# A decoder layer: the first sorted tiles set between the last token tiles, and the last two blocks' first-stage rows added by TensorE

## The chip, the cores and the metric

One core of a Trainium2 chip runs the whole layer in one launch. The metric is the device time of the kernel in microseconds (us). The core has five instruction queues: PE (TensorE, matmuls), DVE (VectorE), ACT (ScalarE), POOL (GpSimd, here mostly the indirect DMAs that scatter rows) and SP (SyncE, the other DMAs). Each runs its instructions in the order in which they are written; semaphores order the queues among each other.

## What is computed

The layer takes 4096 tokens (4 sequences of 1024) with 256 features. Three stages follow one another, each with a residual and a LayerNorm: a gated convolution with a scan (the first stage), three steps of slot attention with a GRU, in which the tokens are the slots, and a mixture of eight experts of which each token uses one:

```python
# GRU cell of the slot attention, three times
    r = jax.nn.sigmoid(xr + hr)
    z = jax.nn.sigmoid(xz + hz)
    n = jnp.tanh(xn + r * hn)
    return (1.0 - z) * n + z * h
...
# experts
    scores = jnp.einsum('bsh,eh->bse', x, gate_w)
    chosen = jnp.argmax(scores, axis=-1)
    onehot = jax.nn.one_hot(chosen, gate_w.shape[0], dtype=x.dtype)
    expert_out = jnp.einsum('bsh,efh->bsef', x, expert_w)
    return x + jnp.einsum('bsef,bse->bsf', expert_out, onehot)
...
    x = _layernorm(x + _L0_attn_ref(x, ...), axis=-1)
    x = _layernorm(x + _L0_xattn_ref(x, ctx_1024, ...), axis=-1)
    x = _layernorm(x + _L0_ffn_ref(x, L0_ffn_gate_w, L0_ffn_expert_w), axis=-1)
```

The second residual is what the change is about: the input of the experts is (first-stage rows + GRU slots), centred and scaled.

## The kernel before

**GRU units.** The slots are kept with features on partitions, in `full` (chunk c of 2, sequence b of 4). A pass k (of six) handles two sequences in eight units q = 0 to 7; a unit is one block of 512 tokens and one chunk of 128 features. For a unit PE runs the hidden and input matmuls of the gates R, HN, XN and Z (`unit`, line 1403), ACT the sigmoids and tanh, and DVE (`hidden_part` 1788, `input_part` 1795, `mix` 1806 to 1817) ends it with the new slots. `LAST` is the last pass; its units 4 and 5 finish block 6 (tokens of tiles 24 to 27), its units 6 and 7 block 7 (tiles 28 to 31). So a block is four token tiles.

**First-stage rows.** They wait in DRAM (`x1_scratch`) and are loaded block by block into the two buffers of `x1b`. The sum with the finished slots is made in place in `full`: for blocks 0 to 3 by POOL (`add_x1`), for blocks 4 to 6 by DVE (`add_block`, line 1892), and for block 7 in two halves, one per feature chunk (`add_half`, line 1900; the half of chunk 0 stands before unit 7 ends, that of chunk 1 behind it). Semaphore `w_mid` counts these sums.

**Token tiles.** `token_tile(n)` (line 1367) turns 128 tokens to rows: two matmuls, one per chunk, against `eyeg`, which holds the identity, the centred gate weights of the eight experts and a column of -1/256. It gives a PSUM bank with 128 + 9 columns per chunk. DVE adds the nine extra columns (`score`, 1839), ACT writes the centred row to `rowb` (`row`, 773) and squares it (`row_square`, 780).

**Sorting.** Tokens come in five groups: tiles 0 to 7, 8 to 15, 16 to 23, 24 to 27 and 28 to 31. Per group DVE picks the expert (`choose`), PE counts ranks (`ranks`, 1383 to 1385), DVE makes addresses (`destinations`, 1871 to 1875), and POOL sends each row by an indirect DMA to its expert's region in DRAM (`send_row`, 1014). After group 2 the first 15 sorted tiles of 128 rows (`NSOON`), filled from the first 24 token tiles alone, can be laid out: `soon_places` gives their rows, and SP gathers them (`gather`, 498) as soon as the rows of groups 0 to 2 have landed. The other 24 tiles need the counts of all groups: `first_counts` to `last_rows`, a chain of dependent small DVE instructions, then `base_set` 2, and the landing of all rows.

**Sorted tiles.** For each of 39 tiles, in order: `turn(i)` (PE transposes a gathered tile into PSUM, 1464), a copy to `wT` (ACT `copy_turned`, 787, for the first 15; DVE `copy_late`, 1997, for the rest), `expert(i)` (two matmuls against the weights of the expert plus identity, 1493, into one of six PSUM buffers), `statistics(i)` on DVE (2001, 2003). For each group of three (`TG`) follow `variance`, `out_index`, ACT's `inverse`, DVE's `offset` (2031), ACT's `normalise` (806), and POOL's `send_out` (1022). A PSUM buffer is free again when its row is normalised, six tiles later.

**The order around the change.** On PE: units 6 and 7 with tiles 24 to 27 inside, `ranks(3)`, tiles 28 to 31, `turn(0)`, then per i: `turn(i + 1)`, `expert(i)`, with `ranks(4)` behind expert(0). On DVE: four scores, `choose(4)`, `statistics(0)`, `destinations(4)`, and the counting chain with statistics 1 and 2 in it, statistics 3 to 5 behind it. On POOL: all 32 row sends, then all 39 output sends. The order is written out by hand; nothing plans it.

## Time and profile before

| | us |
|---|---|
| median of 3 runs | 594.06 |
| lowest, highest | 592.83, 597.93 |
| the profiled execution | 590.11 |
| its span in the trace | 588.3 |
| mean granted TensorE clock in it | 0.945 |

The profiled execution is a separate one; its span runs from the first to the last instruction, and 1.8 us lie around it. Times in the rows are from the span's start.
### The profile page before, as it was taken

The numbers are of one execution on the slowest core, as the hardware profiler recorded it, in microseconds if no ns is written. First come the engines' busy times: TensorE is split into PE (matmuls) and PEld (weight loads), VectorE is DVE, ScalarE is ACT, GpSimd is POOL, SyncE is SP. The second block draws the span as 40 slices with busy tenths as digits, with TensorE's granted clock in tenths as the row PEclk, the third lists the DMA queues.
The fourth block names the chain that finished last, engine by engine and source line by source line (L and its number), as shares of the span: only waits on it lengthen the run. The fifth ranks groups of instructions, "written<-read, shape, count | busy, mean of one in ns | idle before, by whom it ended". The sixth has DMA issues, their size and how long they took to land.

```text
span 588.3 us, 7233 instructions
## 1 busy us (share of the span) xinstructions
PE 519.0 (88%) x2158; PEld 372.4 (63%) x2158; DVE 439.7 (75%) x798; ACT 344.0 (58%) x608; POOL 240.4 (41%) x213
## 2 busy tenths in 40 slices
PE   6999896979779989999999999999899887987770
PEld 2466454737656865787688678768677766765550
DVE  2899999987996679799679859965956767655551
ACT  3657459775884746674676667456476635452322
POOL 0021030302132546559356555915433564564553
PEclk9999997989799989999999999999999988688985
DMA  8950202110001040000000000021121723454410
GB/s 297 297 169 2 72 1 74 70 71 1 37 36 73 0 145 0 2 0 2 0 1 0 1 0 2 0 72 36 36 72 40 270 77 106 132 170 122 135 67 28
DMA packets 28101, 39.98 MB, mean 68 GB/s; under 512 B 7421, under 2 KB 19838, under 8 KB 27776
## 3 DMA queue, kind: packets, MB, share of 16 engines
q1 hardware_dynamic: 24656, 31.10, 17.0%
q0 software_dynamic: 3408, 8.43, 4.0%
q8 instruction: 18, 0.29, 0.2%
q14 instruction: 19, 0.16, 0.1%
HBM read 25.70 MB, written 16.83 MB: 72 GB/s over the span
## 4 chain that ended last, share of the span: by engine, by line
PE 46%; DVE 13%; issue 7%; POOL 2%; another core or an unknown queue 2%; ACT 2%; POOLq 0%; DVEq 0%; ACTq 0%
PE psum L1403 32%; PE psum L1493 6%; PE psum L1234 2%; PE psum L1367 2%; PE psum L1464 2%; DVE gru L1815 2%; DVE slots_full L1817 1%; PE psum L1319 1%; DVE gru L1788 1%; DVE gru L1795 1%; POOL gru L984 1%; DVE slots_lo L1638 1%; PE psum L1331 1%; DVE st L2001 1%
## 5 line engine op out<-in xcount | busy, mean ns | idle before, releaser
L1403 PE MATMUL psum<-slots_hi,w_hh 128*128 128x512 f32 x560 | 182.5, 408 | 4.5 <-DVE gru L1788 4.5
L1403 PEld LDWEIGHTS psum<-slots_hi,w_hh 128*128 128x128 f32 x560 | 104.8, 192 | 32.1 <-DVE gru L1788 5.8
L1403 PE MATMUL psum<-slots_lo,w_hh 128*128 128x512 f32 x280 | 112.5, 402 | 0.0
L984 POOL TENSOR_TENSOR gru<-slots_full,gru 128x512 f32<-128x512 f32 x43 | 65.8, 1530 | 112.8 <-ACT gru L750 112.8
L1403 PE MATMUL psum<-at,v_ih_pair 128*128 128x512 f32 x288 | 92.6, 406 | 3.1 <-DVE at L1694 3.1
L750 ACT ACTIVATE gru<-gru,vec 128x512 f32<-128x512 f32 x48 | 34.6, 722 | 63.7 <-DVE gru L1795 63.5
L1403 PEld LDWEIGHTS psum<-at,v_ih_pair 128*128 128x128 f32 x288 | 54.7, 193 | 19.8 <-DVE at L1694 3.4
L1788 DVE SCALAR_TENSOR_TENSOR gru<-psum,vec,gru 128x512 f32<-128x512 f32 x48 | 35.9, 748 | 39.3 <-PE psum L1403 30.1
L1117 PE MATMUL psum<-early_hi,w_in 128*128 128x512 f32 x128 | 58.6, 618 | 5.1 <-DMA early_hi<-in_xT 5.1
L1403 PEld LDWEIGHTS psum<-slots_lo,w_hh 128*128 128x128 f32 x280 | 53.8, 192 | 12.9
L1493 PE MATMUL psum<-slots_full,w_tile 128*128 x156 | 49.3, 445 | 13.5 <-DVE w_tile L1997 9.2
L1022 POOL DMA_INDIRECT out<-out_tile,out_index x39 | 37.9, 972 | 32.0 <-ACT out_tile L806 19.5
L1117 PEld LDWEIGHTS psum<-early_hi,w_in 128*128 128x128 f32 x128 | 25.3, 199 | 36.0 <-issue 35.1
L1815 DVE TENSOR_TENSOR gru<-gru 128x512 f32<-128x512 f32 x48 | 42.9, 893 | 5.3 <-ACT gru L757 2.2
L999 POOL TENSOR_TENSOR slots_lo<-slots_full,slots_hi 128x512 fp32r<-128x512 f32 x32 | 46.6, 1456 | 0.6 <-DVE slots_hi L1822 0.6
L1817 DVE TENSOR_TENSOR slots_full<-gru 128x512 f32<-128x512 f32 x48 | 45.0, 937 | 1.7
L744 ACT ACTIVATE gru<-psum,brz 128x512 f32<-128x512 f32 x48 | 32.7, 681 | 22.6 <-PE psum L1403 22.4
L1014 POOL DMA_INDIRECT sorted_rows<-row_block,dest x32 | 33.4, 1043 | 27.9 <-DVE row_block L1885 10.4
L1493 PEld LDWEIGHTS psum<-slots_full,w_tile 128*128 128x128 f32 x156 | 30.7, 219 | 21.8 <-issue 18.1
L1795 DVE TENSOR_TENSOR gru<-psum,gru 128x512 f32<-128x512 f32 x48 | 33.2, 692 | 7.5 <-PE psum L1403 5.3
L993 POOL TENSOR_TENSOR ss_block<-sq_block 128x512 f32<-128x512 f32 x16 | 22.3, 1391 | 39.2 <-ACT sq_block L765 35.7
L757 ACT ACTIVATE gru<-psum,brz 128x512 f32<-128x512 f32 x48 | 32.5, 677 | 2.0 <-PE psum L1403 1.8
(239 smaller groups left out, 874.0 us busy)
## 6 DMA issues: line engine op xcount, KB each, us to landing
gathered<-sorted_rows SPq DMA_DIRECT2D x39, 129.0 KB
x_scratch<-slots_full SPq DMA_DIRECT2D x8, 512.0 KB, 3.0
x_block<-x_scratch SPq DMA_DIRECT2D x8, 512.0 KB, 4.0
early_hi<-in_xT SPq DMA_DIRECT2D x3, 1024.0 KB, 5.5
x_tm<-in_x SPq DMA_DIRECT2D x4, 512.0 KB, 7.2
slots_full<-expert_plus SPq DMA_DIRECT2D x1, 2048.0 KB
sorted_rows<-gru SPq DMA_DIRECT2D x1, 1032.0 KB, 11.7
early_hi<-in_xT SPq DMA_DIRECT2D x2, 512.0 KB, 4.3
```

The costliest lines, as they stand in the source:

```text
L750: act.activation(X(u), X(u), ACT.Tanh, bias=col(c, V_BIH + 2)).then_inc(n_act, 1)
L984: pool.tensor_tensor(DF(u), full[:, c, seq(k, h), blk(j)], X(u), ALU.subtract).then_inc(d_pool, 1)
L999: last = pool.tensor_tensor(slots[1][:, c, b, blk(j)], full[:, c, b, blk(j)], slots[0][:, c, b, blk(j)].bitcast(F32), ALU.subtract)
L1014: pool.indirect_dma_start(rows[:], bass.IndirectOffsetOnAxis(dest[:, n:n + 1], 0), rowb[:, row_slot(n), :], None, bounds_check=E * REGION - 1,
L1022: pool.indirect_dma_start(out[:], bass.IndirectOffsetOnAxis(oidx[:, g % 4, t:t + 1], 0), og[:, i % (4 * TG), :], None, bounds_check=TOK - ...
L1117: last = pe.matmul(psum[:, bank + j, :], wi[:, k, at_col:at_col + P], xF[b % 2][:, k, cols_of(j)], start=k == 0, stop=k == C - 1)
L1403: last = pe.matmul(psum[:, bank, :], w, d, start=start and i == 0, stop=stop and i == len(pairs) - 1, skip_group_check=begun or late)
L1493: last = pe.matmul(expert_out(i), wT[:, i % TG, c, :], ew[:, c, bass.ds(off, D)], start=c == 0, stop=c == C - 1)
L1788: dve.scalar_tensor_tensor(out=X(u), in0=psum[:, HN_B, :], scalar=col(c, V_BHH + 2), in1=X(u), op0=ALU.add, op1=ALU.mult).then_inc(t_dve, 1)
L1795: dve.tensor_tensor(X(u), psum[:, XN_B, :], X(u), ALU.add).then_inc(t2_dve, 1)
L1815: dve.tensor_tensor(Z(u), Z(u), DF(u), ALU.mult).then_inc(e_dve, 1)
L1817: dve.tensor_tensor(full[:, c, seq(k, h), blk(j)], X(u), Z(u), ALU.add).then_inc(s_dve, 1)
```

## The change

Four things change together. First, DVE's adds of blocks 6 and 7 go. Tiles 24 to 31 take the first-stage rows by two more matmuls out of `x1b` (`late_input`), accumulated in PSUM with the two out of the unsummed slots (`late_slots`). Second, on PE the input parts of tiles 28 to 31 stand ahead of `ranks(3)`, and their slot parts behind `turn(0)`, between the first sorted tiles; `ranks(4)` moves from behind expert(0) to behind expert(3). The first three gathers get a semaphore each, so that `turn(0)` waits for its own gather alone. Third, ACT and DVE follow this order: copies between the last rows, statistics between the last scores and through the counting chain. Fourth, POOL sends the first three outputs ahead of the rows of tiles 28 to 31.

```diff
@@ block.sync
-                    gather(i, places[i] if i < TG else row_of(i), gat_in[i // TG % 4])
+                    gather(i, places[i] if i < TG else row_of(i), gat_first[i] if i < TG else gat_in[i // TG % 4])
@@ block.scalar, normalise
-                        if g < NE and t < TG - 1 and TG * g + 6 + t < NSOON:
+                        if g == 0:
+                            copy_turned(5 + t)
+                        elif g < NE and t < TG - 1 and TG * g + 6 + t < NSOON:
                             copy_turned(TG * g + 6 + t)
@@ block.scalar
-                for n in range(28, 32):
-                    row(n)
-                copy_turned(0)
+                for i in range(TG):
+                    copy_turned(i)
+                    row(28 + i)
+                row(31)
                 row_square(28)
                 row_square(29)
-                copy_turned(1)
+                copy_turned(3)
                 row_square(30)
                 row_square(31)
-                for i in range(2, 5):
-                    copy_turned(i)
                 inverse(0)
-                copy_turned(5)
+                copy_turned(4)
                 normalise(0)
@@ block.gpsimd
-                for g, (t0, n) in enumerate(GROUPS):
+                def send_group(g):
+                    t0, n = GROUPS[g]
                     for t in range(t0, t0 + n):
                         send_row(t, g)
-                for i in range(NTL):
+
+                for g in range(NGRP - 1):
+                    send_group(g)
+                for i in range(TG):
+                    send_out(i)
+                send_group(NGRP - 1)
+                for i in range(TG, NTL):
                     send_out(i)
@@ block.tensor
+                def late_input(n):
+
+                    i = n // TJ
+                    pe.wait_ge(x1_in3[i % 2], 16 * (i // 2 + 1))
+                    token_bank(n)
+                    for c in range(C):
+                        pe.matmul(token_part(n, c), x1b[:, i % 2, c, token_cols(n, TJ)], eyeg[:, c, :],
+                                  start=c == 0, stop=False, skip_group_check=True)
+
+                def late_slots(n):
+                    b, i = n // NT, n // TJ
+                    for c in range(C):
+                        pe.wait_ge(s_dve, UL - QU + C * i + (c + 1 if i == 2 * B - 1 else C))
+                        last = pe.matmul(token_part(n, c), full[:, c, b, token_cols(n, NT)], eyeg[:, c, :],
+                                         start=False, stop=True, skip_group_check=True)
+                    last.then_inc(tile_mm, 1)
@@ block.tensor, turn
-                    if g == NE:
-                        pe.wait_ge(gat_first[t], 16)
+                    if g in (0, NE):
+                        pe.wait_ge(gat_first[t], 16 if g == 0 else 32)
@@ block.tensor
-                unit(LAST, 6, {"XN": tiles_after(24)})
-                token_tile(25)
-                unit(LAST, 7, {"R": tiles_after(26), "HN": tiles_after(27)})
+                unit(LAST, 6, {"XN": late_after(24)})
+                late_tile(25)
+                unit(LAST, 7, {"R": late_after(26), "HN": late_after(27)})
+                for n in range(28, 32):
+                    late_input(n)
                 ranks(3)
-                token_tile(28)
-                token_tile(29)
-                token_tile(30)
-                token_tile(31)
                 turn(0)
                 for i in range(NSOON):
                     off = offset_of(i)
+                    if i < TG:
+                        late_slots(28 + i)
+                    if i == TG - 1:
+                        late_slots(31)
                     if i + 1 < NSOON:
                         turn(i + 1)
                     expert(i, off)
-                    if i == 0:
+                    if i == TG:
                         ranks(4)
@@ block.vector
                 settle(LAST, 5)
-                add_block(6)
                 hidden_part(LAST, 6)
...
                 mix(LAST, 6, soon_passed)
-                add_half(0)
                 score(25)
...
                 settle(LAST, 7)
-                add_half(1)
                 destinations(3)
                 side(3)
-                for n in range(28, 32):
-                    score(n)
+                score(28)
+                statistics(0)
+                score(29)
+                statistics(1)
+                score(30)
+                score(31)
                 choose(4)
...
                 variance(0)
                 out_index(0)
-                last_counts(link)
+                side(4)
                 offset(0)
+                statistics(3)
+                destinations(4)
+                statistics(4)
+                first_counts(link)
+                statistics(5)
...
```

`token_tile` keeps its form for tiles 0 to 23; its waits for banks move unchanged into `token_bank(n)`, which `late_input` calls. `late_after(n)` and `late_tile(n)` run `late_input(n)` and `late_slots(n)` one behind the other. In the rest of DVE's new order `variance`, `out_index` and `offset` of groups 1 and 2 and statistics 6 to 8 stand between the parts of the counting chain, whose instructions are the same.

PE behind the last unit, before. `slots_full` with `eye_and_gate` is a token tile, `gathered` a turn, `w_tile` an expert.

```order
L1367 MATMUL psum<-eye_and_gate,slots_full 128x137 [waits t_dve,w_mid]
L1367 MATMUL psum<-eye_and_gate,slots_full 128x137
L1367 MATMUL psum<-eye_and_gate,slots_full 128x137 [waits t2_dve,w_mid]
L1367 MATMUL psum<-eye_and_gate,slots_full 128x137
L1464 MATMUL psum<-ident,gathered 128x128 [waits r_act,gat_in_0]
L1464 MATMUL psum<-ident,gathered 128x128
L1475 TENSOR_LOAD soon_off [waits more_set]
L1464 MATMUL psum<-ident,gathered 128x128 [waits turn_ev]
L1464 MATMUL psum<-ident,gathered 128x128
L1493 ISA [waits z_act,ew_in,turn_ev]
L1493 ISA x2
L1493 MATMUL psum<-slots_full,w_tile 128x256
```

After; `x1_block` is an input part (1391), `slots_full` with `eye_and_gate` a slot part (1398).

```order
L1420 MATMUL psum<-cum4_1,ones_f 128x32
L1499 MATMUL psum<-ident,gathered 128x128 [waits r_act,gat_first_0]
L1499 MATMUL psum<-ident,gathered 128x128
L1510 TENSOR_LOAD soon_off [waits more_set]
L1398 MATMUL psum<-eye_and_gate,slots_full 128x137 [waits s_dve] x2
L1499 MATMUL psum<-ident,gathered 128x128 [waits turn_ev,gat_first_1]
L1499 MATMUL psum<-ident,gathered 128x128
L1528 ISA [waits z_act,ew_in,turn_ev]
L1528 ISA x2
L1528 MATMUL psum<-slots_full,w_tile 128x256
L1528 ISA x2
L1528 MATMUL psum<-slots_full,w_tile 128x256
```

The turn of tile 0 has come ahead of all slot parts of tiles 28 to 31, and expert(0) stands behind one of them where it stood behind four tiles.

DVE behind the last row's side columns, before. `token_scores` is a score, `route_tmp`, `hot4` and `cum4` the choice, `st3` and `mv3` statistics.

```order
L1883 COPY row_block<-tok 128x4 [waits row_out_0]
L1885 TENSOR_SCALAR row_block<-ssq 128x4 [waits sq_ev]
L1839 TENSOR_REDUCE token_scores<-psum 128x9 [waits tile_mm] x4
L1853 TENSOR_REDUCE mx<-token_scores 128x4 [waits score_ev]
L1854 TENSOR_TENSOR route_tmp<-token_scores,mx 128x32 [waits route]
L1855 TENSOR_TENSOR route_tmp<-route_tmp,order 128x32 [waits route]
L1856 TENSOR_REDUCE mx<-route_tmp 128x4 [waits route]
L1857 TENSOR_TENSOR hot4_0<-route_tmp,mx 128x4x8 [waits route]
L1862 COPY hot4_0<-cum4_1 128x8 [waits route]
L1864 SCALAR_TENSOR_TENSOR cum4_0<-reset4,hot4_0 128x40 [waits route]
L2001 BN_STATS st3<-psum 128x6 [waits y_mm,route]
L2003 BN_AGGR mv3<-st3 128x2 [waits bn_done]
```

After, from the same place.

```order
L1927 TENSOR_SCALAR row_block<-ssq 128x4 [waits sq_ev]
L1881 TENSOR_REDUCE token_scores<-psum 128x9 [waits tile_mm]
L2035 BN_STATS st3<-psum 128x6 [waits y_mm]
L2037 BN_AGGR mv3<-st3 128x2 [waits bn_done]
L1881 TENSOR_REDUCE token_scores<-psum 128x9 [waits tile_mm]
L2035 BN_STATS st3<-psum 128x6 [waits y_mm]
L2037 BN_AGGR mv3<-st3 128x2 [waits bn_done]
L1881 TENSOR_REDUCE token_scores<-psum 128x9 [waits tile_mm] x2
L1895 TENSOR_REDUCE mx<-token_scores 128x4 [waits score_ev]
L1896 TENSOR_TENSOR route_tmp<-token_scores,mx 128x32 [waits route]
L1897 TENSOR_TENSOR route_tmp<-route_tmp,order 128x32 [waits route]
L1898 TENSOR_REDUCE mx<-route_tmp 128x4 [waits route]
```

Two statistics have come between the scores, so the last two scores and the choice stand behind expert(1).

The end of POOL's queue, before; `sorted_rows` is a row send, `out` an output send.

```order
L1008 TENSOR_TENSOR slots_full<-slots_full,x1_block 128x2x512 x2
L984 TENSOR_TENSOR gru<-slots_full,gru 128x512 x3
L1014 DMA sorted_rows<-row_block,dest 33920x258 x32
L1022 DMA out_0<-out_tile,out_index 4096x256 x39
L411 UNCONDITIONAL_BRANCH
```

After.

```order
L985 TENSOR_TENSOR gru<-slots_full,gru 128x512 x3
L1015 DMA sorted_rows<-row_block,dest 33920x258 x28
L1023 DMA out_0<-out_tile,out_index 4096x256 x3
L1015 DMA sorted_rows<-row_block,dest 33920x258 x4
L1023 DMA out_0<-out_tile,out_index 4096x256 x36
```

Three output sends have come ahead of the last four row sends.

## Rows read from the trace of the kernel before

**Rows 1.** The page: the span, then part 1.

```profile
span 588.3 us, 7233 instructions
PE 519.0 (88%) x2158; PEld 372.4 (63%) x2158; DVE 439.7 (75%) x798; ACT 344.0 (58%) x608; POOL 240.4 (41%) x213
```

**Rows 2.** Timeline of DVE, 480 to 502: start us, us, what, [idle before <-releaser].

```profile
480.29 0.69 DVE L1817 TENSOR_TENSOR slots_full<-gru 128x512 f32<-128x512 f32 x1
481.09 1.23 DVE L1892 TENSOR_TENSOR slots_full<-slots_full,x_block 128x1024 f32<-128x1024 f32 x1
482.23 0.75 DVE L1788 SCALAR_TENSOR_TENSOR gru<-psum,vec,gru 128x512 f32<-128x512 f32 x1
...
496.45 0.69 DVE L1900 TENSOR_TENSOR slots_full<-slots_full,x_block 128x512 f32<-128x512 f32 x1
...
501.25 0.18 DVE L1839 TENSOR_REDUCE token_scores<-psum 128x9 f32<-128x18 f32 x1 [0.74 <-issue]
```

**Rows 3.** Timeline of PE, 478 to 528.

```profile
482.37 1.28 PE L1367 MATMUL psum<-eye_and_gate,slots_full 128*128 128x137 f32 x4 [2.87 <-DVE slots_full L1892]
...
486.25 0.63 PE L1367 MATMUL psum<-eye_and_gate,slots_full 128*128 128x137 f32 x4
...
497.20 4.02 PE L1367 MATMUL psum<-eye_and_gate,slots_full 128*128 128x137 f32 x16 [2.34 <-DVE slots_full L1900]
...
502.82 2.07 PE L1493 MATMUL psum<-slots_full,w_tile 128*128 x4
...
523.55 1.03 PE L1493 MATMUL psum<-slots_full,w_tile 128*128 x4
...
527.82 0.60 PE L1464 MATMUL psum<-ident,gathered 128*128 128x128 f32 x4
```

**Rows 4.** Windows: us, each engine's busy time, granted clock, DMA share, GB/s.

```profile
483.00:485.00 2.00, 2.00 (x7) 1.71 (x7) 1.54 (x8) 0.82 (x2) 1.39 (x3) 0.50 0.18 66
497.00:501.00 4.00, 3.80 (x16) 3.81 (x17) 1.30 (x9) 1.40 (x3) 1.94 (x2) 0.50 0.66 172
501.40:521.20 19.80, 17.25 (x68) 13.06 (x67) 13.12 (x63) 10.11 (x32) 10.35 (x11) 0.76 0.49 141
505.00:509.00 4.00, 4.00 (x15) 3.44 (x16) 2.55 (x14) 0.72 (x2) 1.22 (x2) 0.50 0.05 16
```

**Rows 5.** SP timeline, 440 to 494; DMA activity in 40 slices of 488 to 498; landings.

```profile
493.61 0.38 SPq L498 DMA_DIRECT2D gathered<-sorted_rows  x1
...
GB/s 0 0 0 0 0 248 281 0 0 0 0 231 297 0 0 0 215 297 17 0 0 0 0 0 0 0 50 198 264 198 248 161 153 190 120 54 116 272 124 78
...
x_block<-x_scratch SPq DMA_DIRECT2D x8, 512.0 KB, 4.0
...
eye_and_gate<-in_gateT SPq DMA_DIRECT2D x1, 8.0 KB, 2.2
```

**Rows 6.** Timeline of POOL, 490 to 520.

```profile
490.60 0.97 POOL L1014 DMA_INDIRECT sorted_rows<-row_block,dest  x1 [0.30 <-issue]
...
511.31 0.97 POOL L1014 DMA_INDIRECT sorted_rows<-row_block,dest  x1 [0.30 <-DVE out_index L2021]
513.42 0.97 POOL L1022 DMA_INDIRECT out<-out_tile,out_index  x1 [1.14 <-issue]
```

**Rows 7.** Timeline of ACT, 498 to 518.

```profile
501.46 0.47 ACT L773 ACTIVATE row_block<-psum,token_scores 128x256 f32<-128x256 f32 x1 [0.44 <-DVE token_scores L1839]
501.84 0.38 ACT L787 ACTIVATE w_tile<-psum 128x256 f32<-128x256 f32 x1
...
512.06 0.56 ACT L806 ACTIVATE out_tile<-psum,nm,rs 128x256 f32<-128x256 f32 x1 [0.42 <-DVE nm L2031]
```

**Rows 8.** Timeline of DVE, 503 to 533.

```profile
506.05 0.19 DVE L1871 TENSOR_TENSOR route_tmp<-psum,hot 128x32 f32<-128x32 f32 x1 [0.28 <-PE psum L1385]
...
521.22 0.16 DVE L2031 SCALAR_TENSOR_TENSOR nm<-mv,rs 128x3 f32<-128x3 f32 x1 [0.59 <-ACT rs L796]
```

**Rows 9.** Waits of DVE, 480 to 589: us in total, times, longest.

```profile
DVE w_tile L1997 <- remote: 7.6, 4, 3.1
```

73 lines of the change are left out of this document (38 added, 35 removed).

## The prediction

> **What bounds the kernel now.** I read the page first: over the whole span PE is busy for 88%, DVE for 75% [rows 1]. That average says little, since the change touches only the hand-over from the last recurrent units to the sorted tiles (480 to 528 us of the trace). So I took the timelines of that stretch, engine by engine, then the granted clock by windows.
>
> At 480.98 us (480.29 + 0.69) DVE has finished the slots of block 6, and spends 1.23 us on adding the first-stage rows to it before the next unit's hidden part at 482.23 [rows 2]. PE sits for 2.87 us in front of token tile 24, until 482.37 [rows 3], and comes back at 0.50 of its clock, the 1.2 GHz level [rows 4]. The same happens for block 7: the slots are ready just before 496.45, the second half add starts there, and PE begins tiles 28 to 31 at 497.20 after 2.34 us of idleness. It takes 4.02 us for them, 1.0 each, at half clock [rows 3, 4]. The last score ends at 501.43 (501.25 + 0.18). Only then do the sorted tiles begin: expert(0) runs 502.82 to 504.89 [rows 3], although its gather was issued at 493.61 [rows 5]. DVE then finds the last ranks at 506.05, goes through the tile counts, and reaches the offset of output group 2 at 521.22 [rows 8]; expert(11), whose PSUM buffer is freed by that group, starts at 523.55 [rows 3]. Between 501.4 and 521.2 DVE is busy for 13.12 of 19.80 us [rows 4]: this is the path that I follow. From expert(11) on, instructions and order are those of before.
>
> **1. The first-stage rows added on TensorE.** Three DVE adds go: one of 1.23 us and two halves of 0.69 us (one stands in the rows), 2.61 us in all [rows 2]. Each of eight token tiles gets two more matmuls, so a full-clock 0.35 us or so more (a whole tile of two matmuls spans 0.63, four of them on end less each) and 0.5 to 1.0 us at half clock [rows 3]. What is gained up to the last slots: the first add gives 1.2 (482.23 against 481.05); the half add at block 6 gives 0.7; and since PE fills its 2.87 us with the input part of tile 24 and resumes at 481.05, it waits for about 1.1 us, less than half of before, and may keep the full clock. Two units' gates stand behind it, for which half clock costs up to 1.5 us (3 us of matmuls at half clock, of which 483 to 485 stands in [rows 4], are 1.5 at full). From this goes the extra matmul work of tiles 24 to 27, 4 x 0.35 = 1.4 us, partly in idle time. Bounds 1.6 and 2.8 us; I take 2.3, so the last slots are there at 494.0 and not 496.35.
>
> **2. What is late next: the first gather.** The tensor queue is in order, and turn(0) now stands ahead of the slot part of tile 28. It waits for gather 0. SP issues that at 493.61 because it waited for token rows 16 to 23, whose last send ended at 491.57 (490.60 + 0.97) [rows 5, 6]; nothing in the change moves either. Its landing is not in the trace. The DMA activity (slices of 0.25 us from 488) starts at 494.5 and has moved 129 KB by 495.25 [rows 5]. An 8 KB load lands 2.2 us after issue, a 512 KB one after 4.0 [rows 5], so between 495.8 and 497.6; I take 496.0, being near the small one. So of the 3.1 us between 497.20 and the new 494.1 only some 0.7 are kept by tile 28.
>
> The Trainium skill, page "DMA: Bandwidth & Descriptors", section "Anatomy of one DMA", puts the fixed part of a DMA at about 2.0 us and the rest at bytes over 436 GB/s. By that the gather would land at 495.9, as an estimate, and the sum would be 0.1 us better; the landing of 2.2 us for 8 KB agrees. By this rule the change puts a fixed 2 us in front of the slot parts, where before it lay behind the last tiles.
>
> **3. The interleaving.** From 496.0 at half clock, with 0.5 per turn, 0.5 per half token tile (half of 1.0 [rows 3]) and 2.0 per expert [rows 3]: turn(0) 496.5; slots of 28 497.0, beside the copy of 0.38 on ACT [rows 7]; turn(1) 497.5; expert(0) 499.5; slots of 29 500.0; turn(2) 500.5; expert(1) 502.5; slots of 30 and 31 503.5. So expert(0) ends 5.4 us earlier than before and the last score, at 503.7, 2.3 us later. Expert(2) needs row 30 out of bank 4 (0.47 on ACT [rows 7]) and turn(3): 504.0 to 506.0. Expert(3) to 508.0; ranks(4), now behind it, about 1.1; destinations(4) at 509.2 against 506.05 [rows 8], 3.1 later.
>
> **4. POOL's queue.** Three output sends now stand ahead of the sends of rows 28 to 31. The first waits for expert(2)'s statistics (506.7), variance, root and offset (some 1.4) and the 0.56 of the output row [rows 7]: 508.7. Three sends at a pitch of 1.28 (511.31 to 513.42 is longer, its own work 0.97 plus 0.30 [rows 6]) bring rows 28 to 31 to 512.5 and their end to 517.4, against 512.28 (511.31 + 0.97): 5.1 later. Two more for landing (491.57 to 493.61) and gather 15 is issued at 519.4, landed by 521.8. Who waits for it is turn(15), at 527.82 before [rows 3] and wanted at 524.7 by the sum below: 2.9 us of slack. So I cost this at nothing; without that slack it costs one for one.
>
> **5. DVE's path to expert(11).** DVE has the same counting to do, mixed with the statistics of tiles 3 to 8. It has less after the last score, as statistics 0 and 1 (some 0.6 each) lie ahead of it: 13.12 - 1.2 = 11.9 us. Hand-offs between some 56 instructions at 0.03 are 1.7. Of the 5 us in which it waited (mainly for expert(0) and expert(1) at half clock) I leave 1.8, for expert(2), the four row squares on ACT and three roots. 503.7 + 15.4 = 519.1, against 521.22: 2.1 earlier. Expert(11) follows with the offset 0.16, the output row 0.56 and hand-offs, at 520.4: before, PE itself came later than its buffer. 523.55 - 520.4 = 3.1, of which I count 3.0, the rest being shared with the wait for statistics.
>
> **Sum.** -3.0 us. The profiled execution took 590.11 us (span 588.3 and 1.8 around it), so this gives 587.1; the three timed runs have their median at 594.06, 4 us above the profiled one, and I take the same 3.0 off it: 591.0 us. Alone, with half clock for 3 us more or less and the landing between its bounds, 589.3 to 592.8.
>
> **Rivals.** (a) *TensorE gets its full clock back at once.* In the new order PE is packed where it had gaps of 0.6 us and more. Then a turn costs 0.3, an expert 1.05 [rows 3] and a half tile 0.25; the slots of 31 end at 500.3, the last score at 500.5, 3.2 earlier than in my sum, and all behind it moves along: -6.0, 588.1 us. Against it: the stretch 505 to 509 was busy for 4.00 of 4.00 us and still at 0.50 [rows 4]. The Trainium skill, page "TensorE: Matmul & The Clock Gate", Part 1 on the HAM clock gate, says the slow state is the default and activity releases it; by that rule the denser stretch is the faster one, and this is the rival it gives. The trace bears it out in part only.
>
> (b) *The half clock lasts longer.* With PE slow until 512, experts 4 to 6 cost 2.4 instead of 1.3 each and eat what DVE gained: -0.5, 593.5 us. For it, PE idles for 2 us ahead of turn(0) as it did ahead of tile 28.
>
> (c) *Slower: DVE's unexplained stops grow.* In this stretch the copies of turned tiles waited four times for something outside the profile's semaphores, 7.6 us in total, the longest 3.1 [rows 9]. I found them beside POOL's longer runs of sends. In the new order POOL has a backlog from 508.7 on, with no pause in a dozen sends and more. If that brings two more stops at 2.75 on the path to expert(14), the sum is -3.0 + 5.5 = +2.5: 596.6 us. It decides from the second added stop on. Against it: the sends up to 491.57 [rows 6] also ran on end, and no such stop stands beside them.
>
> (d) *The change does not reach the end*, since turn(15) waits for gather 15. This needs 2.9 us more than point 4 has; for 3 us beyond it the time is 594.
>
> **Chances.** Forecast 0.48, (a) 0.22, (b) with (d) 0.14, (c) 0.16. A measurement here tells about 1% from no change, that is 5.9 us. Below 588.1 lie half of (a) and a tail of cases in which the clock also holds at 482, 0.25 together; above 600.0 lie 0.08, the worse part of (c); within 1% 0.67. The range goes from just beyond (a) to (c): 586.5 to 597.0.
>
> **What would show it.** Right: PE resumes at the slots of block 6 with a clock near 1.00 in the four microseconds behind; the last slots come some 2.3 us before 496.35; turn(0) waits for its gather, not for slots; the last score comes later than before and expert(0) some 5 us earlier; expert(11) some 3 us earlier; turn(15) waits for no gather. Wrong: gather 15 ending PE's wait; a granted clock of 1.00 from 500 on (then (a)); DVE's "remote" stops at the copies well above 7.6 us in all (then (c)); or a tail behind expert(11) that is not as long as before, which I hold fixed at 588.3 - 523.55 = 64.75 us.

## The result, and the profile after

The changed kernel takes 593.75 us (median of 20 runs, 591.11 to 596.41), the kernel before 591.93 us (20 runs). The ratio is 1.0048, with a 95% interval of 1.0026 to 1.0069: 2.8 us slower, where 3.0 us faster was forecast. The time is inside the range, and on the wrong side of no change. The two medians lie only 1.8 us apart; the ratio, by which I go throughout, is taken over the fast executions alone.

Most times below are counted from one instruction, the end of the slots of block 6 on DVE: 480.98 us before (480.29 + 0.69), 482.80 after. All that lies ahead of it is the same program, and it moves by 1 to 2 us from execution to execution. I call such a time +x. The marks that recur are the last slots (the end of the slots of block 7), the last score, the last ranks in DVE's hands (with them the sorting of the last tiles begins), the offset of output group 2, and the start of expert(11).

The page of the changed kernel, as [rows 1]:

```profile
span 592.8 us, 7294 instructions
PE 519.6 (88%) x2190; PEld 373.2 (63%) x2190; DVE 437.7 (74%) x795; ACT 343.8 (58%) x608; POOL 239.3 (40%) x213
```

DVE's timeline, as [rows 2, 8]:

```profile
482.11 0.69 DVE L1859 TENSOR_TENSOR slots_full<-gru 128x512 f32<-128x512 f32 x1
...
497.24 0.69 DVE L1859 TENSOR_TENSOR slots_full<-gru 128x512 f32<-128x512 f32 x1
...
505.15 0.18 DVE L1881 TENSOR_REDUCE token_scores<-psum 128x9 f32<-128x18 f32 x1 [2.00 <-remote]
...
510.88 0.19 DVE L1913 TENSOR_TENSOR route_tmp<-psum,hot 128x32 f32<-128x32 f32 x1 [0.47 <-PE psum L1420]
...
513.06 0.43 DVE L2035 BATCH_NORM_STATS2 st<-psum 128x6 f32<-128x256 f32 x1 [1.55 <-PE psum L1528]
...
523.61 0.16 DVE L2065 SCALAR_TENSOR_TENSOR nm<-mv,rs 128x3 f32<-128x3 f32 x1 [0.43 <-issue]
526.70 0.43 DVE L2035 BATCH_NORM_STATS2 st<-psum 128x6 f32<-128x256 f32 x1 [2.92 <-remote]
```

No add stands behind the slots of block 6 any more. The last slots end at 497.93, +15.1, where before had +15.4. The last score ends at +22.5 (before +20.4), the last ranks are in DVE's hands at 510.88, +28.1 (before +25.1), the offset of output group 2 begins at +40.8 (before +40.2). Behind it comes a stop of 2.92 us that nothing in the profile explains.

PE, as [rows 3]:

```profile
482.86 0.74 PE L1398 MATMUL psum<-eye_and_gate,slots_full 128*128 128x137 f32 x4 [1.15 <-DVE slots_full L1859]
...
496.48 0.44 PE L1499 MATMUL psum<-ident,gathered 128*128 128x128 f32 x2
...
497.99 0.50 PE L1398 MATMUL psum<-eye_and_gate,slots_full 128*128 128x137 f32 x2 [0.49 <-DVE slots_full L1859]
...
501.15 1.10 PE L1398 MATMUL psum<-eye_and_gate,slots_full 128*128 128x137 f32 x8
...
504.34 1.43 PE L1528 MATMUL psum<-slots_full,w_tile 128*128 x4 [1.87 <-ACT row_block L773]
507.16 0.69 PE L1499 MATMUL psum<-ident,gathered 128*128 128x128 f32 x2 [1.38 <-ACT w_tile L787]
507.64 2.07 PE L1528 MATMUL psum<-slots_full,w_tile 128*128 x4
...
527.28 0.66 PE L1499 MATMUL psum<-ident,gathered 128*128 128x128 f32 x2 [4.27 <-ACT w_tile L787]
527.79 2.07 PE L1528 MATMUL psum<-slots_full,w_tile 128*128 x4
```

PE's stop ahead of tile 24 has shrunk from 2.87 to 1.15 us. turn(0) runs at 496.48 without a wait. PE has done the slot parts of tiles 30 and 31 at 502.25 (501.15 + 1.10), +19.5, which is 0.8 us earlier than before (+20.2). But DVE takes the last score 2.9 us later, at 505.15, after a stop of 2.00 us that no known semaphore ends. So the last score is late by that stop, and not by PE. From 504 on PE waits twice: expert(2) 1.87 us for row 30, which has to leave expert(2)'s bank of PSUM, and turn(4) 1.38 us for ACT's copy of tile 3, which stands behind the squares of rows 28 and 29. Expert(11), right behind turn(12), begins at 527.79, +45.0; before it was +42.6. From its start to the end of the span it is 65.0 us, against 64.75. So the whole loss is there when expert(11) starts.

Windows, as [rows 4]:

```profile
483.00:485.00 2.00, 2.00 (x11) 1.73 (x12) 1.85 (x8) 0.34 (x1) 1.47 (x2) 1.00 0.31 114
490.00:494.00 4.00, 4.00 (x24) 3.46 (x23) 1.74 (x6) 0.87 (x3) 1.95 (x2) 1.00 0.27 99
497.00:501.00 4.00, 3.48 (x20) 2.97 (x21) 2.28 (x11) 2.01 (x6) 1.27 (x2) 1.00 0.54 137
505.00:509.00 4.00, 2.62 (x8) 1.53 (x7) 2.83 (x15) 3.42 (x14) 0.00 (x0) 0.50 0.28 81
501.40:521.20 19.80, 15.38 (x62) 11.65 (x60) 11.47 (x52) 8.60 (x27) 9.03 (x10) 0.74 0.39 116
```

The clock (the number behind the busy times) stands at 1.00 in the three windows between 483 and 501, where before had 0.50 in 483 to 485 and in 497 to 501. It is at 0.50 in 505 to 509: it falls behind the first of PE's two waits. In 490 to 494 PE is busy for 4.00 of 4.00 us.

Two engines more, POOL and ACT:

```profile
520.23 0.97 POOL L1015 DMA_INDIRECT sorted_rows<-row_block,dest  x1 [0.30 <-issue]
```

```profile
523.14 0.20 ACT L794 ACTIVATE rs<-mv 128x3 f32<-128x3 f32 x1 [1.37 <-DVE mv L2047]
...
526.75 0.38 ACT L787 ACTIVATE w_tile<-psum 128x256 f32<-128x256 f32 x1 [3.17 <-remote]
```

POOL's sends of rows 28 to 31, of which this is the last, end at 521.20. ACT's copy of tile 11, the one that expert(11) needs, stands behind the two steps of the root of group 2 (the first at 523.14, the second ends at 523.58), and then waits 3.17 us more for nothing that the profile knows, up to the moment at which DVE's stop ends too. POOL's sends of rows 24 to 27 lie earlier, from 499.42 to 504.23, beside the stop ahead of the last score.

### The profile page after: what moved, and what is told of

It reads as the page before. It is cut to its first block, busy times and chain, and to the rows that moved or that the text cites. A ratio compares the mean times of both kernels' runs of the same rounds, so it can differ in the third digit from the quotient of the medians.

```text
span 592.8 us, 7294 instructions
## 1 busy us (share of the span) xinstructions
PE 519.6 (88%) x2190; PEld 373.2 (63%) x2190; DVE 437.7 (74%) x795; ACT 343.8 (58%) x608; POOL 239.3 (40%) x213
## 4 chain that ended last, share of the span: by engine, by line
PE 48%; DVE 10%; issue 7%; POOL 2%; another core or an unknown queue 2%; ACT 2%; POOLq 0%; DVEq 0%; ACTq 0%
PE psum L1438 33%; PE psum L1528 6%; PE psum L1242 2%; PE psum L1499 2%; DVE gru L1857 1%; PE psum L1327 1%; DVE slots_full L1859 1%; PE psum L1381 1%; POOL gru L985 1%; DVE gru L1830 1%; DVE gru L1837 1%; PE psum L1398 1%; POOL slots_lo L1000 1%; PE psum L1339 1%
## 5 line engine op out<-in xcount | busy, mean ns | idle before, releaser
L1438 PEld LDWEIGHTS psum<-slots_hi,w_hh 128*128 128x128 f32 x560 | 104.0, 191 | 34.3 <-DVE gru L1830 8.6
L1438 PE MATMUL psum<-at,v_ih_pair 128*128 128x512 f32 x288 | 90.9, 400 | 3.1 <-DVE at L1736 3.1
L1528 PE MATMUL psum<-slots_full,w_tile 128*128 x156 | 51.6, 461 | 12.1 <-issue 6.8
```

The lines of the kernel that those rows point to most:

```text
L1438: last = pe.matmul(psum[:, bank, :], w, d, start=start and i == 0, stop=stop and i == len(pairs) - 1, skip_group_check=begun or late)
L1528: last = pe.matmul(expert_out(i), wT[:, i % TG, c, :], ew[:, c, bass.ds(off, D)], start=c == 0, stop=c == C - 1)
```

## The experiments

Eighteen runs of seventeen kernels. The ratio is always to the kernel before on the same chip; 0.001 is 0.6 us. Each trace is one execution, so a mark in it can be off by more than the differences that it is used for; where the ratio and a mark disagree, the ratio counts.

### Half of the change at a time: adds_only, order_only

adds_only is the kernel before with TensorE's adds in its own order. Condensed from the edit (tiles 24 to 27 become `late_tile` as well):

```diff
-                add_block(6)            # and add_half(0), add_half(1)
-                token_tile(28)          # to 31, behind ranks(3)
+                for n in range(28, 32):
+                    late_input(n)
+                ranks(3)
+                for n in range(28, 32):
+                    late_slots(n)
```

> The kernel before with only the first half of the change: the first-stage rows of blocks 6 and 7 are added by TensorE in token tiles 24 to 31, the three DVE adds go, and the order of before stays (slots of 28 to 31, then turn(0), ranks(4) behind expert(0)). Theory A, the new order is what cost 2.8 us (ratio 1.0048 for the whole change): this half alone is worth nothing or a little, ratio 0.998 to 1.001, and the last slots come 15.1 us after the slots of block 6, as in the trace after. Theory B, the eight extra pairs of matmuls eat more than the adds gave: ratio 1.003 to 1.006. Theory C, my step 1 was right and only this execution hid it: -2.3 us, ratio 0.996.

order_only is the changed kernel with the three DVE adds and whole tiles put back (`late_slots(28 + i)` becomes `token_tile(28 + i)`).

> The changed kernel with the DVE adds put back (block 6 and the two halves of block 7) and whole token tiles 24 to 31 at the places where the changed kernel has their slot parts; so the new order alone. Theory A, the order costs the time: ratio 1.004 to 1.008, the offset of output group 2 no earlier than 40.8 us after the slots of block 6. Theory B, the matmuls cost the time: ratio 0.998 to 1.001. If both halves cost something, 1.002 to 1.004 in each.

Measured: adds_only 0.9948 (0.9914 to 0.9982), that is 3.1 us faster; order_only 1.0045 (1.0015 to 1.0076). The order is what costs, as theory A says. But the adds are worth more than A allowed (0.998 to 1.001): their ratio is the one that theory C gave (0.996), although C's reason, earlier last slots, does not appear in the trace. On top of the adds the order costs more, 0.010, since the adds' gain goes as well. Of adds_only I show DVE and PE:

```profile
480.73 0.69 DVE L1849 TENSOR_TENSOR slots_full<-gru 128x512 f32<-128x512 f32 x1
...
495.86 0.69 DVE L1849 TENSOR_TENSOR slots_full<-gru 128x512 f32<-128x512 f32 x1
...
498.55 0.18 DVE L1871 TENSOR_REDUCE token_scores<-psum 128x9 f32<-128x18 f32 x1 [0.29 <-issue]
```

```profile
492.34 2.21 PE L1383 MATMUL psum<-eye_and_gate,x_block 128*128 128x137 f32 x16
...
496.61 1.91 PE L1390 MATMUL psum<-eye_and_gate,slots_full 128*128 128x137 f32 x14 [1.23 <-DVE slots_full L1849]
```

The last slots come at +15.1, no earlier than after the whole change and 0.3 us earlier than before. The last score comes at +17.3 (before +20.4). The eight first halves of tiles 28 to 31 are done in the 2.21 us from 492.34, while DVE and ACT finish the last unit, and at full clock the slot parts need 1.91 us instead of 4.02 [rows 3]. That is where the adds pay: behind the last slots, not ahead of them.

### Its repetition: adds_again

The same kernel.

> The same kernel as adds_only once more, for a second trace and more runs. If its ratio of 0.9948 holds, this one falls within 0.992 to 0.998; if the true gain is nearer to nothing, it comes to 0.998 or above. In the trace the last slots come 15.1 us after the slots of block 6 and the last score 17.3 us after them (20.5 in the kernel before), since the first halves of tiles 28 to 31 are done by then. If stops of DVE and ACT belong to places of the program, they stand where they stood (504.6, 508.3, 526.2, 548.9, 564.8 us, within 1 us); if they are of the moment, they stand elsewhere.

Measured: 0.9962 (0.9938 to 0.9987), 2.2 us faster; slots at +15.0, last score at +17.2. ACT's unexplained stops end at 503.5, 507.1 and 525.5 (in adds_only at 504.6, 508.3 and 526.2); DVE's two at 549.0 and 564.8 in adds_only, of 3.74 and 3.37 us, have no counterpart of that kind. So some of them belong to places of the program, and some don't.

### Followers put back one by one: pool_back, copy3_first, counts_first, interleave_only

pool_back has `for g in range(NGRP): send_group(g)` ahead of all `send_out(i)`.

> The changed kernel with POOL's queue as before: the sends of rows 28 to 31 ahead of all output sends. Theory P, the late row sends (end at 521.20 in the trace after, gather 15 issued only at 526.6) are what costs: the ratio falls to 0.999 to 1.001 and gather 15 is issued some 4 us earlier. Rival: nobody waits for gather 15, as turn(15) comes at 534.2, so the ratio stays at 1.004 to 1.006.

Measured 1.0054 (1.0026 to 1.0082): the order of POOL's sends is not what costs in this kernel.

copy3_first moves two copies on ACT:

```diff
                 row(31)
+                copy_turned(3)
                 row_square(28)
                 row_square(29)
-                copy_turned(3)
                 row_square(30)
                 row_square(31)
-                inverse(0)
                 copy_turned(4)
+                inverse(0)
```

> The changed kernel with one thing moved on ACT: the copy of turned tile 3 stands right behind row 31, ahead of the squares of rows 28 and 29, and the copy of turned tile 4 ahead of inverse(0). Theory Q, PE's idle time between 505 and 508 us (expert(3) waits for that copy, and the clock then falls to 0.50) is what costs: expert(3) starts 1.0 to 1.4 us earlier, less half clock in 508 to 515, and 1.5 to 2.5 us of the loss come back, ratio 1.000 to 1.002. Rival: the chain through the last score, ranks(4) and the counts sets the time, and the ratio stays within 0.001 of 1.0048.

Measured 1.0022 (0.9993 to 1.0052). Expert(3) starts at +23.9 instead of +24.8 and at full clock, and expert(11) at +44.0 instead of +45.0. The ratio is below the change's 1.0048, but the interval reaches from no gain to all of it. In the one trace the gain at expert(11) is gone by the end: 67.4 us from there to the end of the span, against 65.0.

counts_first has all counting (destinations(4), first_counts to last_rows) ahead of statistics(3).

> The changed kernel with DVE's counts back ahead of the statistics of tiles 3 to 8 (statistics 0 to 2 stay between the scores); PE, ACT and POOL as in the changed kernel. counts_mixed says that the mixing alone cost 0.009. Theory D: the ratio falls from 1.0048 to 0.998 to 1.001, base_set 2 comes 3 us or more earlier than 522.1 us. Rival: with ranks(4) behind expert(3) the counts start too late in any order, and the ratio stays at 1.003 to 1.007.

Measured 1.0031 (1.0005 to 1.0058); expert(11) at +43.8. The counts were through at +34.3 instead of +40.1 (the last of their instructions is `gru<-gru,i_col`), so the edit did what it should, and yet expert(11) came only 1.2 us earlier. The ratio lies at the lower edge of the rival's 1.003 to 1.007, but its interval holds the upper edge of theory D too.

interleave_only puts all of these back at once, with ranks(4) behind expert(2). It keeps the adds and the interleaving on PE, and what belongs to it on the other engines: the copies between the last rows on ACT, and statistics 0 and 1 between the last scores on DVE.

> The changed kernel with all followers of the interleaving put back at once: counts ahead of the statistics, POOL's row sends ahead of its output sends, the copy of tile 3 ahead of the squares, ranks(4) behind expert(2). What stays is the change's core: TensorE adds, and experts 0 to 2 between the slot parts of 28 to 31. Theory F, the followers carry the loss: 0.993 to 0.997, as adds_only. Rival G, the interleaving itself costs, since the last score comes 23 us after the slots of block 6 and not 17.3: 0.999 to 1.004.

Measured 1.0022 (0.9998 to 1.0047), clearly above adds_only. Rival G: the interleaving (with ranks(4) two experts later than in adds_only) costs by itself. The last score comes at +20.8 instead of +17.3.

In all kernels with the interleaving DVE takes the last score late. Where the order of before stands, it ends 0.2 us behind PE's last slot part, in all of these traces. In the whole new order it ends 3.0 to 3.2 us behind it, in all five (the change, pool_back, copy3_first, counts_first, after_no_out), and in interleave_only and order_only 1.6 and 1.7 us. copy3_first shows it plainly, as the score before the last comes in time:

```profile
500.64 0.18 DVE L1881 TENSOR_REDUCE token_scores<-psum 128x9 f32<-128x18 f32 x1 [0.32 <-PE psum L1398]
503.53 0.18 DVE L1881 TENSOR_REDUCE token_scores<-psum 128x9 f32<-128x18 f32 x1 [2.71 <-remote]
```

In the changed kernel PE's last slot part ends at +19.5, 2.4 us later than in adds_only (+17.1): so much is the interleaving, and the rest of the 5.2 us is the stop. POOL sends rows 24 to 27 in that stretch (499.42 to 504.23). Whether these sends cause it was not tried.

### Single pieces laid onto adds_only: pool_late, ranks_late, counts_mixed

Each is adds_only with one piece of the new order: POOL's queue; `if i == TG: ranks(4)` instead of `if i == 0`; DVE's list behind choose(4).

> The kernel with the TensorE adds in the order of before (adds_only, ratio 0.9948), and of the new order only POOL's part: the sends of output tiles 0 to 2 ahead of the sends of rows 28 to 31. If POOL's part carries the loss, the ratio comes to 1.001 to 1.005. If, as pool_back said, POOL's queue is not it, it stays within 0.001 of 0.9948; the sends of rows 28 to 31 then end some 9 us later than in adds_only and gather 15 as much later, with turn(15) not waiting.

> adds_only with one line moved: ranks(4) behind expert(3), as in the changed kernel, and not behind expert(0). Theory R, the routing chain (last score, ranks(4), destinations(4), counts, offset 2, the gathers from 15 on) carries the loss: destinations(4) comes 4 to 6 us later and the ratio rises to 1.000 to 1.005. Rival: the counts have slack behind the statistics, and it stays within 0.002 of 0.9948.

> adds_only with DVE's list of the changed kernel behind choose(4): statistics 3 to 8 mixed with destinations(4) and the counts, where before the counts ran ahead. Theory D, the mixing carries the loss, as the counts now stand behind experts 3 to 8: base_set 2 comes 3 to 7 us later than 514 us, ratio 1.000 to 1.005. Rival: TensorE's order alone does, and it stays within 0.002 of 0.9948.

Measured: pool_late 1.0009 (0.9969 to 1.0050), ranks_late 0.9978 (0.9934 to 1.0022), counts_mixed 1.0041 (0.9998 to 1.0083). Against 0.9948 they cost some 3.6, 1.8 and 5.5 us, each give or take 3. So counts_mixed comes out as its theory D said and pool_late at the edge of what was expected if POOL's part carried the loss; ranks_late lies between its two, and can't be told from adds_only. Together that is more than the 5.9 us which the order costs as a whole, so the pieces don't simply add up, unless it is the noise of three such differences. pool_late surprised me, as pool_back had acquitted POOL. Its one trace runs ahead of adds_only up to 514 us and then loses all of it in one stop, here on ACT (DVE's ends at 519.11, after 4.78 us):

```profile
521.26 0.38 ACT L787 ACTIVATE w_tile<-psum 128x256 f32<-128x256 f32 x1 [6.52 <-remote]
```

POOL was by then in a run of nine sends on end (first and last of them):

```profile
509.03 0.97 POOL L1022 DMA_INDIRECT out<-out_tile,out_index  x1 [7.70 <-ACT out_tile L806]
...
519.25 0.97 POOL L1022 DMA_INDIRECT out<-out_tile,out_index  x1 [0.30 <-issue]
```

### What the stops are: more_records, many_records, one_expert

The stops hit kernels that were ahead harder than those that were behind, so they could have been a limit on instructions. more_records and many_records add waits on SP that are long satisfied:

```diff
+                        for _ in range(4):     # 12 in many_records, there from gather 3 on
+                            sp.wait_ge(corner_set, 1)
+                            sp.wait_ge(plus_out, 16 * (C + 1))
                         gather(i, ...)
```

> The kernel before with eight more waits on SP, all on semaphores that were set long before, ahead of each gather from 15 on (192 more instructions, some 0.05 us each on a queue that is idle most of the time). It is for the stops of 2 to 4 us in which DVE and ACT wait for nothing that the profile shows. Theory S, the stops follow from how many instructions all engines put through in the microseconds before them: the stops behind 520 us grow by 4 us or more in all and the ratio is above 1.005. Rival: they have nothing to do with it, ratio 0.999 to 1.001.

> more_records made stronger: 24 waits that are long satisfied (12 instructions) ahead of each gather from 3 on, some 430 instructions where all engines together put through about 1,580 behind 490 us. SP needs 1.4 us for a gather instead of 0.8, still less than the 1.8 us at which tiles are consumed. Theory S, the stops are a limit on how many instructions go through (in the profile): 27% more of them cost 8 us or more, ratio above 1.012. Rival: nothing, 0.999 to 1.003.

more_records: 1.0015 (0.9976 to 1.0055), nothing that can be told. (Two waits make one instruction, so it had 96 more and not 192.) many_records: 1.0285 (1.0236 to 1.0335), 16.8 us slower, as theory S asked for. But it proves nothing. These are two of its waits from 510 us on:

```profile
PE psum L1470 <- DMA gathered<-sorted_rows: 15.3, 6, 4.1
DVE st L2007 <- remote: 3.7, 1, 3.7
```

PE waited 15.3 us for gathers: I had made SP the bottleneck, whereas the unexplained waits shrank. Why a gather took longer than the 1.4 us that I had put down was not looked into.

one_expert is adds_only without PE's register load and address arithmetic per sorted tile: `ew[:, c, bass.ds(off, D)]` becomes `ew[:, c, 0:D]`, so that every tile takes the weights of expert 0.

> adds_only with the expert's weights always taken from expert 0, without TensorE's register load and address arithmetic of each sorted tile (the choice of the expert is left out, so the output is not the reference's). Theory T, the stops belong to TensorE's register loads or to its instruction count (some seven instructions less per sorted tile of about 40 of all engines): they go or halve, time 4 us or more under adds_only. Theory V: the stops at runs of POOL's sends stay as they are, and the time falls by 0 to 3 us.

Measured: 0.9904 (0.9866 to 0.9941), 0.004 to 0.006 under the adds, or 2.6 to 3.4 us where theory T asked for 4 or more. The stops stay (waits from 510 us on, as the profile sums them up):

```profile
DVE w_tile L2021 <- remote: 4.0, 3, 3.1
ACT w_tile L787 <- remote: 3.4, 1, 3.4
DVE st L2025 <- remote: 2.3, 1, 2.3
```

### Without POOL's output sends: before_no_out, adds_no_out, after_no_out

The edit is the same in all: the sends of output tiles 0 to 35 go, and the waits for them, so that most of the output is not written.

```diff
                 def send_out(i):
+                    if i // TG < NG - 1:
+                        return
```

> The kernel before without the sends of output tiles 0 to 35 and the waits for them; only the last output group is sent, so most of the output is not written. Theory V, the stops of DVE and ACT belong to POOL's long runs of sends: those behind 525 us (2.9, 1.2, 3.1, 2.4 us) are gone and the time falls by 6 to 12 us. Rival S, they belong to the number of instructions of all engines or to TensorE's own: two or more stops of 2 us remain behind 515 us and the time falls by less than 4 us (the last sends are still waited for).

> adds_only without the sends of output tiles 0 to 35 (most of the output is not written). Theory V: no stop over 1.5 us behind 515 us, and against before_no_out the gain of the TensorE adds is whole, 2 to 3 us. Rival S: stops remain, gain as in adds_only.

> The changed kernel without the sends of output tiles 0 to 35 (most of the output is not written). Theory V, the loss of the new order sits in the stops that POOL's sends bring: it is then no slower than adds_no_out (within 0.003 of it). Theory R, the loss sits in the routing chain (last score, counts, gather 15) and PE's idle time between 504 and 520 us: it stays 4 to 6 us slower than adds_no_out.

Measured: 0.9623 (0.9581 to 0.9666), 0.9547 (0.9515 to 0.9579) and 0.9632 (0.9599 to 0.9665); 569.70, 565.96 and 570.45 us. In none of the three is a wait marked "remote" left behind 510 us. Of the stops behind 510 us theory V is right, and the fall goes well beyond what it said (22.3 us for the kernel before, against 6 to 12). Waits for buffers and half of the DMA traffic went with the sends, so this is what the sends cost, and not the stops alone. Windows of adds_only and of adds_no_out show the difference:

```profile
530.00:555.00 25.00, 18.81 (x86) 14.31 (x85) 13.92 (x53) 7.55 (x20) 12.56 (x14) 0.93 0.46 135
```

```profile
530.00:555.00 25.00, 25.00 (x122) 19.34 (x121) 21.45 (x85) 12.44 (x34) 0.00 (x0) 1.00 0.24 65
```

PE is busy for 25.00 of 25.00 us instead of 18.81, with 122 groups of instructions instead of 86. That also ends theory S: many more instructions per us go through, and nothing stops.

Of the loss theory V is wrong and theory R right in its size: without a stop behind 510 us the new order is still 4.5 us slower than the adds alone. Three instructions of DVE in each trace (slots of block 6, last score, variance of group 2), first of before_no_out, then adds_no_out, then after_no_out:

```profile
481.50 0.69 DVE L1816 TENSOR_TENSOR slots_full<-gru 128x512 f32<-128x512 f32 x1
...
501.79 0.18 DVE L1838 TENSOR_REDUCE token_scores<-psum 128x9 f32<-128x18 f32 x1 [0.74 <-issue]
...
520.79 0.17 DVE L2012 TENSOR_TENSOR mv<-mv,gathered 128x3 f32<-128x3 f32 x1
```

```profile
481.63 0.69 DVE L1848 TENSOR_TENSOR slots_full<-gru 128x512 f32<-128x512 f32 x1
...
499.46 0.18 DVE L1870 TENSOR_REDUCE token_scores<-psum 128x9 f32<-128x18 f32 x1 [0.29 <-issue]
...
518.10 0.17 DVE L2036 TENSOR_TENSOR mv<-mv,gathered 128x3 f32<-128x3 f32 x1
```

```profile
480.53 0.69 DVE L1858 TENSOR_TENSOR slots_full<-gru 128x512 f32<-128x512 f32 x1
...
503.65 0.18 DVE L1880 TENSOR_REDUCE token_scores<-psum 128x9 f32<-128x18 f32 x1 [1.31 <-remote]
...
521.43 0.17 DVE L2046 TENSOR_TENSOR mv<-mv,gathered 128x3 f32<-128x3 f32 x1
```

From the end of the slots of block 6, the variance of group 2 starts at +38.6, +35.8 and +40.2. ACT's root of that group and the copy of turned tile 11 wait for it, and PE for the copy (ACT, then PE, of after_no_out):

```profile
521.63 0.20 ACT L793 ACTIVATE rs<-mv 128x3 f32<-128x3 f32 x1 [2.94 <-DVE mv L2046]
```

```profile
522.49 0.41 PE L1498 MATMUL psum<-ident,gathered 128*128 128x128 f32 x2 [2.58 <-ACT w_tile L786]
523.00 1.13 PE L1527 MATMUL psum<-slots_full,w_tile 128*128 x4
```

Ahead of 510 us, beside POOL's sends of rows 24 to 27 and just behind them, stops do remain, and they hit different instructions. In after_no_out PE is done with the slot parts at 500.68 (this row), and the last score ends 3.1 us later:

```profile
499.81 0.87 PE L1397 MATMUL psum<-eye_and_gate,slots_full 128*128 128x137 f32 x6
```

In adds_no_out the last score is through by then (it ends 0.2 us behind PE), and the stop falls on the next thing that DVE takes from PE, the ranks, 2.1 us behind PE's records of them:

```profile
504.80 0.19 DVE L1902 TENSOR_TENSOR route_tmp<-psum,hot 128x32 f32<-128x32 f32 x1 [1.74 <-remote]
```

Both stops end at nearly the same mark, +22.4 and +22.5. So the chains that are compared here aren't free of stops; they differ by some 1 us in them, of the 4.5.

Expert(11) starts at +40.4, +37.4 and +41.8, and from there the three spans end after 44.8, 44.6 and 44.6 us. The differences at expert(11), -3.0 and +1.4, are those of the times, -3.7 and +0.8, within 0.7 us.

### Which piece, without the output sends: interleave_no_out, counts_mixed_no_out

> interleave_only without the sends of output tiles 0 to 35 (most of the output is not written), to be compared with adds_no_out (565.96 us, ratio 0.9547) and after_no_out (570.45 us, 0.9632). Theory R: what counts is when variance(2) is ready, since the copy of turned tile 11 stands behind inverse(2) on ACT. The interleaving puts the last score 5 us later (22.6 against 17.3 us behind the slots of block 6); ranks behind expert(2) and the counts ahead of the statistics leave 1 to 3 us of that: 567 to 569 us. Rival F, the interleaving is harmless by itself and the followers carry the loss: 565 to 566.5 us.

> counts_mixed without the sends of output tiles 0 to 35 (most of the output is not written). The last score is as early as in adds_no_out; the counts stand among the statistics. Theory R: destinations(4) waits behind statistics(3), some 4 us later than in adds_no_out, but DVE then has no statistics left over, and variance(2) comes 1 to 4 us later than there: 567 to 570 us. Rival: the mixing fills DVE's idle time, 564 to 566 us, and the loss of counts_mixed with all sends (0.009) came from the stops.

Measured: 0.9671 (0.9633 to 0.9708) and 0.9615 (0.9578 to 0.9652), on another chip (568.87 and 566.58 us there). Against 0.9547 both cost. The marks at the slots of block 6, in us:

```
kernel                 last score   variance(2)   expert(11)   from there to the end
before_no_out            +19.8         +38.6         +40.4          44.8
adds_no_out              +17.3         +35.8         +37.4          44.6
counts_mixed_no_out      +17.1         +37.5         +39.1          45.7
interleave_no_out        +20.9         +37.9         +40.5          44.7
after_no_out             +22.6         +40.2         +41.8          44.6
```

By the ratios each piece takes back most or all of what the adds gain (0.0076). By the marks it is 1.7 and 3.1 us of 3.0; the trace of counts_mixed_no_out is the slowest of its six executions and that of interleave_no_out the fastest of its six, so the table makes the interleaving look cheaper than it is. In counts_mixed_no_out DVE's destinations of the last rows stand behind the statistics of experts 1, 2 and 3, and those experts haven't run when DVE gets there (it waits 1.89 us for expert 1, this row, and 1.65 for expert 2):

```profile
504.29 0.43 DVE L2024 BATCH_NORM_STATS2 st<-psum 128x6 f32<-128x256 f32 x1 [1.89 <-PE psum L1519]
...
509.54 0.17 DVE L1906 CAST dest<-mx 128x4 int32<-128x4 f32 x1
```

The cast of the destinations, the last row, begins at +27.5; in adds_no_out, where only one statistics stands ahead, it begins at 505.26, +22.9.

In interleave_no_out the last score is late, and with the counts ahead, the variance of group 1 is late, for which ACT waits 4.05 us here, and PE then 3.25 us for ACT:

```profile
513.14 0.21 ACT L793 ACTIVATE rs<-mv 128x3 f32<-128x3 f32 x1 [4.05 <-DVE mv L2043]
```

With the sends in place the picture is similar, blurred by the stops. Expert(11) starts at +40.4 and +40.0 (adds_only, adds_again), +41.3 (ranks_late), +42.6 (before), +42.9 (interleave_only), +43.8 (counts_first, counts_mixed), +44.0 (copy3_first), +44.6 (pool_late), +45.0 (the change), +46.3 (pool_back), +46.4 (order_only). But for pool_late that is roughly the order of the ratios, 0.995 to 1.005. What lies behind expert(11) is less fixed here: in these twelve traces it takes 63.2 to 67.4 us.

## Why the prediction was wrong, step by step

**What bounds it.** Right in the main: the path runs from the last score over the counts and group 2 to expert(11), and what lies behind is fixed in the pair (65.0 against 64.75 us; 44.6 to 44.8 in three kernels without sends). In the other traces with sends it moves by 4 us.

**Step 1 (adds).** The clock was kept, as said (1.00 in 483 to 485). The gain was not: some 0.3 us up to the last slots, not 2.3, and over all traces 14.7 to 16.4 us with DVE's adds against 14.9 to 15.2 with TensorE's. The term that failed is "4 x 0.35 = 1.4 us, partly in idle time". PE is busy without a pause in 490 to 494; an input part costs 0.47 there (PE's timeline has its start at 488.11 and the next one's at 488.58), and behind PE, choose(3) holds DVE as before. The gain came in behind the slots instead, where I had counted it as lost: 3.1 us at the last score in adds_only.

**Step 2 (gather 0).** Wrong: "what is late next: the first gather" isn't. turn(0) ran at 496.48 without a wait, 2.1 us behind the issue at 494.4. The slot part of tile 28 waited for DVE's last slots (0.49 us). The Trainium skill, page "DMA: Bandwidth & Descriptors", section "Anatomy of one DMA", gives 2.0 us plus the bytes over 436 GB/s, for a DMA that GpSimd issues; by that the 129 KB of a gather would take 2.3 us, as an estimate. This gather is issued by SP, and landed within 2.1 us, a little sooner.

**Step 3 (interleaving).** The last score comes 2.1 us later, as forecast (2.3), and destinations(4) 3.0 later (3.1). That the numbers fit is luck, for the way was another. PE ran at full clock, not half, and was done with the last slot part at +19.5, 0.8 us earlier than before; the last score was then late by the stop of 2.00 us ahead of it, which comes again in every trace of this order. Behind it the ranks were late by row 30's bank and by the copy of tile 3 behind two squares. Rival (a) had the clock right and the consequence wrong: the Trainium skill, page "TensorE: Matmul & The Clock Gate", Part 1, has activity release the throttled clock, and the packed stretch 497 to 501 was indeed at 1.00; it saved nothing at the last score, since the stop stood behind it.

**Step 4 (POOL).** "I cost this at nothing" held in the changed kernel (pool_back; turn(15) at 534.22 waits for nothing, although gather 15 was issued only at 526.6). It may not hold in general: on adds_only the same order costs 3.6 us, give or take 3, and its one trace shows a longer run of sends and a longer stop. I had looked for who waits for the rows, and not for what the run does to others.

**Step 5 (DVE's path).** This is the step that failed, with the output sends and without them. I gave DVE 15.4 us from the last score to the offset of group 2; it took 18.3 (505.33 to 523.61), and 18.3 again in after_no_out. "DVE has the same counting to do" was right, and DVE was busy for 11.47 us in 501.4 to 521.2 [rows 4 had 13.12]. What I took away and wasn't gone is the waiting: the term "of the 5 us in which it waited I leave 1.8". It waited 4.4 us in this stretch. In the new list the counts stand behind the statistics of experts 3 to 5, and these run late and at half clock: DVE's timeline has it waiting 1.13 us for the statistics of expert 3, 0.47 for the ranks behind it, and 1.55 for expert 4, up to 513.06, and 0.69, 0.43 and 0.16 at other places; later the statistics that the counts had held back came on top. I counted waits that go, not what is late next in the list. These 2.9 us (18.3 less 15.4) eat the forecast gain of 3.0 and bring it to about no change.

**The tail to expert(11).** "Hand-offs, at 520.4", 1.3 us behind the offset, came to 4.2, with the stop of 3.17 us on ACT's copy. In this pair of traces that is the other half of the miss.

**Sum.** Forecast -3.0 at expert(11), found +2.4 in this pair of traces: 2.9 us from step 5 and 2.9 from the tail, less 0.4 in small things. Without the output sends it is +1.4 in place of -3.0; there, too, step 5 is the largest part. So most of the miss stands without the output sends, and some 1 us goes with them, though one trace of each is little for that. What the stop at the last score takes from it was not measured.

**Rivals.** (c) had the sign and nearly the size (+2.5) and half of the reason: the stops behind 510 us do belong to POOL's output sends. It was not the mechanism that decided: the order loses 4.5 us to the adds with no stop behind 510 us. And its reading of [rows 9] was off: the four stops there end at 532.67 us and later, behind expert(14), and before the change no wait of DVE or ACT is marked "remote" in 495 to 527. In the new order one stands at the last score, at the head of the chain, where the rival had not looked for it. (d) and the wait for gather 0 didn't come up. (b) came nearest to the chain: half clock and DVE's gain eaten.

## What to carry to other kernels

Where one engine works off two chains, a list that serves the earlier result first delays the one that others wait for: find the last score, or whatever heads the longest chain, and let nothing of the next stage stand ahead of it or of its followers. A sum over removed waits needs, for each, the name of what the engine will wait for instead. And when a noisy cost (here POOL's output sends) covers a difference of 1%, take it away in all versions and compare those: three such runs showed that most of the loss stands without it. Then ask which stops are left: those beside the row sends were, and were not taken away.

The version that beats both kernels is adds_only: TensorE adds the first-stage rows, order as before, 3.1 and 2.2 us faster than the kernel before in two series.
